# Order of the query and key loads on SP's line, and the row length of these loads, in a two-block transformer kernel on one core

## What is computed

```python
q = jnp.einsum('oc,bct->bot', Wq, target) + bq[None, :, None]
k = jnp.einsum('oc,bcs->bos', Wk, source) + bk[None, :, None]
v = jnp.einsum('oc,bcs->bos', Wv, source) + bv[None, :, None]
q = q.reshape(b, HEADS, HEAD_DIM, t)
...
dot = jnp.einsum('bhdt,bhds->bhts', q, k) / math.sqrt(HEAD_DIM)
dot = mask * dot - (1.0 - mask) * NEG
amap = jax.nn.softmax(dot, axis=-1) * mask
out = jnp.einsum('bhts,bhds->bhdt', amap, v)
...
x = x + jnp.tanh(g_xattn[0]) * out
```

## Time and profile before

| | us |
|---|---|
| median of 3 runs (1378.74 to 1382.11) | 1381.76 |
| the profiled execution | 1371.15 |
| its span | 1369.3 |
| PE busy / DVE busy / ACT busy / POOL busy | 1113.3 / 1033.2 / 668.1 / 523.4 |
| DMA queue of SP, share of 16 engines over the span | 38.8% |
| attention, about | 158 to 645 |

### The profile page before, as it was taken

One profiled execution on the slowest core, in us unless ns is written; L12 is line 12 of the kernel. 1 busy time (PEld: TensorE's weight loads), 2 busy tenths in 40 slices (PEclk: granted clock), 3 DMA queues, 4 the chain that ended last, 5 costly groups with the idle time before them and its releaser, 6 DMA issues. The chain is left out here.

```text
span 1369.3 us, 16346 instructions
## 1 busy us (share of the span) xinstructions
PE 1113.3 (81%) x4725; PEld 447.5 (33%) x4802; DVE 1033.2 (75%) x1587; ACT 668.1 (49%) x783; POOL 523.4 (38%) x384
## 2 busy tenths in 40 slices
PE   0887279998879987983799998599999999259777
PEld 0443112222222222220344444344444444134232
DVE  5765488887767877751799997388788887767898
ACT  0355308776657766684466665211000000386796
POOL 0466601244332442355011111477888787000021
PEclk9999659999989999997999999799999999579889
DMA  7398797677756776621311110111111111000011
GB/s 266 127 338 319 199 146 83 119 153 108 125 90 124 151 111 115 114 71 58 151 47 46 40 36 16 35 62 62 62 62 50 58 62 46 1 0 0 0 62 62
DMA packets 84274, 129.33 MB, mean 94 GB/s; under 512 B 13544, under 2 KB 53864, under 8 KB 83696
## 3 DMA queue, kind: packets, MB, share of 16 engines
q1 hardware_dynamic: 84224, 128.72, 38.8%
HBM read 104.44 MB, written 21.89 MB: 92 GB/s over the span
## 5 line engine op out<-in xcount | busy, mean ns | idle before, releaser
L793 DVE TENSOR_REDUCE mneg<-ps_m 128x1 f32<-128x512 f32 x512 | 322.2, 683 | 93.8 <-PE ps_m L707 78.3
L1337 PE MATMUL ps_y<-kv,toeplitz_sb 128*128 128x512 f32 x640 | 279.6, 596 | 8.7 <-POOL kv L1249 8.7
L675 ACT ACTIVATE probs<-ps_s 128x1024 f32<-128x1024 f32 x256 | 249.9, 1022 | 51.9 <-PE ps_s L728 51.9
L707 PE MATMUL ps_m<-k_stack,q_stack 128*128 128x512 bf16 x489 | 181.9, 410 | 55.3 <-DMA k_stack<-mask_k 50.4
L1337 PEld LDWEIGHTS ps_y<-kv,toeplitz_sb 128*128 128x128 f32 x640 | 121.1, 191 | 155.0 <-issue 155.0
L728 PE MATMUL ps_s<-q_stack,k_stack 128*128 128x512 bf16 x492 | 151.0, 387 | 21.1 <-ACT probs L675 11.2
L738 PE MATMUL ps_o<-probs,v_all 128*17 128x512 f32 x1024 | 140.1, 620 | 0.4 <-ACT probs L675 0.4
L1249 POOL TENSOR_TENSOR kv<-vT,ctxT_sb 128x2048 f32<-128x2048 f32 x32 | 118.7, 3711 | 40.0 <-PE ps_y L1337 32.6
L972 PE MATMUL ps_g<-w,xT_f 128*128 128x512 bf16 x491 | 116.7, 384 | 8.4 <-DVE h_f L1119 6.6
L623 POOL TENSOR_TENSOR inv_all<-inv_all,mb_b 128x512 f32<-128x512 f32 x16 | 20.4, 1274 | 254.9 <-DMA inv_all<-inv_rows 254.9
L707 PEld LDWEIGHTS ps_m<-k_stack,q_stack 128*128 128x128 bf16 x512 | 42.2, 99 | 219.4 <-DVE mneg L793 104.5
(11 more groups left out here) (163 smaller groups left out, 1662.6 us busy)
## 6 DMA issues: line engine op xcount, KB each, us to landing
w_sweep<-in_w SPq DMA_DIRECT2D x8, 1536.0 KB, 8.5
q_stack<-q_parts SPq DMA_DIRECT2D x96, 128.0 KB
k_stack<-k_parts SPq DMA_DIRECT2D x96, 128.0 KB
w_sweep<-in_w SPq DMA_DIRECT2D x16, 768.0 KB, 6.5
w_sweep<-in_w SPq DMA_DIRECT2D x16, 512.0 KB, 3.3
toeplitz_sb<-in_toeplitz SPq DMA_DIRECT2D x32, 256.0 KB, 2.6
w_f<-in_w SPq DMA_DIRECT2D x32, 256.0 KB, 2.9
q_parts<-qk_part SPq DMA_DIRECT2D x24, 256.0 KB, 4.0
```

The lines of the kernel that those rows point to most:

```text
L675: nc.scalar.activation(pr[:, k % 2, 2 * slot:2 * slot + 2, :], S[:, 2 * slot:2 * slot + 2, :], ACT.Exp).then_inc(exp_done, 1)
L707: nc.tensor.matmul(M[:, bank(j), :], Q[:, slot, hd, tc * P:(tc + 1) * P], K[:, slot, hd, :], start=True, stop=True).then_inc(max_mm, 1)
L793: nc.vector.tensor_reduce(mneg[:, h, tile % LT, tile // LT:tile // LT + 1], M[:, bank(j), :], AX.X, ALU.max, negate=True).then_inc(max_red, 1)
L1337: mm = nc.tensor.matmul(Y[:, q % 3, l2, :], T[:, g % 2, (lt - m) * P:(lt - m + 1) * P], kv[:, g % 2, m, :], start=(m == 0), stop=(m == lt))
```

## The change

Two things. First, SP no longer issues the load of unit u+2 at the start of unit u's turn; at the end of unit u's turn it issues that of unit u+3. The prologue now loads units 0, 1 and 2, the last between the two weight loads. SP's loop over batches is written out instead of run as a loop. Second, the host orders the columns of `wqT` and `wkT` and the biases so that within each 128 channels the channel of head h and dimension d is 8d + h instead of 16h + d. A partition's eight heads then lie in `q_parts` as one run of 8 KB, and a block's load reads 16 such runs; before it read 128 rows of 1 KB. What lies in `Q` and `K` afterwards is the same.

```diff
@@ load_unit
-                                         s.rearrange("a (h d) l -> d (a h) l", d=HD)).then_inc(qk_loaded[slot], 16)
+                                         s.rearrange("a (d h) l -> d (a h) l", d=HD)).then_inc(qk_loaded[slot], 16)
...
                 load_batch(0, 0)
                 load_weights(0, 0)
+                load_unit(1, 2, 0, fresh=True)
                 load_weights(1, 1)
-                sp.wait_ge(zeroed[2], 2)
-                sp.wait_ge(zeroed[3], 2)
                 place_max(0, 0, 0)
...
                 def batch(b, par, first, last):
                     for h in range(2):
                         u = 2 * b + h
-                        if not last:
-                            if not first:
-                                sp.wait_ge(scores_done, 2 * STEPS * (u - 1))
-                            load_unit(b + 1, 2 * (1 - par) + h, h)
...
                             load_weights(u + 1, 1 - h)
+                        if u + 3 < 2 * B:
+                            if u:
+                                sp.wait_ge(scores_done, 2 * STEPS * u)
+                            load_unit((u + 3) // 2, (u + 3) % 4, (u + 3) % 2, fresh=u == 0)
...
-                over_batches(sp, batch)
+                for b in range(B):
+                    batch(b, b % 2, b == 0, b == B - 1)
...
+    def by_dim(v):
+        return np.ascontiguousarray(v.reshape(v.shape[:-1] + (CT, P // HD, HD)).swapaxes(-1, -2).reshape(v.shape))
...
-        "wqT": np.ascontiguousarray(inputs["L0_xattn_Wq"].T), "wkT": np.ascontiguousarray(inputs["L0_xattn_Wk"].T),
+        "wqT": by_dim(inputs["L0_xattn_Wq"].T), "wkT": by_dim(inputs["L0_xattn_Wk"].T),
```

More of the change, by code:

```diff
@@ L1810 @@
         "x": arr("x"), "ctx": arr("ctx_2048"), "mask": arr("mask_Bx1x2048_fk1"), "g_xattn": arr("g_xattn"),
-        "g_ffn": arr("g_ffn"), "bq": columns(inputs["L0_xattn_bq"]), "bk": columns(inputs["L0_xattn_bk"]),
+        "g_ffn": arr("g_ffn"), "bq": columns(by_dim(inputs["L0_xattn_bq"])), "bk": columns(by_dim(inputs["L0_xattn_bk"])),
         "mask_cols": np.ascontiguousarray(inputs["mask_Bx1x2048_fk1"].reshape(B, LT, P).transpose(2, 0, 1)),
         "bv": arr("L0_xattn_bv"),
-        "wqT": np.ascontiguousarray(inputs["L0_xattn_Wq"].T), "wkT": np.ascontiguousarray(inputs["L0_xattn_Wk"].T),
+        "wqT": by_dim(inputs["L0_xattn_Wq"].T), "wkT": by_dim(inputs["L0_xattn_Wk"].T),
         "wvT": np.ascontiguousarray(inputs["L0_xattn_Wv"].T),
```

## The result

The changed kernel takes 1394.12 us (median of 4 runs, 1387.31 to 1398.13), the kernel before 1381.22 on the same chip (median of 4, 1378.74 to 1382.11): a ratio of 1.0091 with a 95% interval of [1.0049, 1.0133]. It is slower, by 12.9 us of medians. The profiled execution took 1387.31 us, the shortest of the four, with a span of 1385.5, against 1371.15 and 1369.3: 16.2 us between the spans. Where they lie is read in order of time.

What follows compares the result with a forecast made beforehand. No engine is full; PE waits for unit loads, up to 48 us. Terms +7.6 - 1.0 + 1.7 + 0 = +8.3 took 1371.15 to 1379.4, 1390 us carried to the median; range 1384 to 1397, 8-in-10 1368 to 1412.

Steps and rivals of the forecast that it cites:

- its own signs of being wrong: Forecast wrong if the load's rate leaves 115 to 130 GB/s, or the prologue's wait is under 4 us.
- From unit 3's load on, no DMA of SP passes another. Price: nothing.: SP's order: only unit 2's load really moves, in the prologue; later order, issue and the written-out loop cost nothing.
- The wait for unit 0's maxima, +7.6: Before unit 0's first scores: PE waits 7.6 us for maxima queued behind unit 2's load, seen at 212.3 against 204.75.
- 1.70 MB at the 121 GB/s of unit 0's and 1's loads: Prologue: unit 2's load, ahead of unit 0's maxima, takes 14.1 us at this rate, so rings are empty at 210.6.
- covered: Rival, chance 0.12: unit 0's maxima find free rings, leaving only -1.0 us, 1381 us; against it, masks and weights use every ring.
- Unit 0's wait for unit 2's load gone, -1.0: In unit 0: the wait at 216.59 vanishes, its step of 3.82 us becoming 2.81, a gain of 1.0 us.
- The clock, +1.7: Behind PE's wait before unit 0's scores: the clock drops as after waits above 2.2 us, costing 1.7 us.
- Rows of 8 KB, 0: In every unit's load: the span of 16 partitions limits the rate, so longer rows change nothing, 0 us.
- rows were the limit: Rival, chance 0.06: in the loads, 8 KB rows take 9.3 us off each, total -58.5 us, 1323 us.
- rows help a little: Rival, chance 0.17: in the loads, engines drift over more blocks, -0.9 us a load, total -8.6 us, 1373 us.
- Rows hurt: Rival, chance 0.17: in the loads, coarser packets put all engines in one block, +1.6 us each, total +40.8, 1423 us.
- The shift is kept.: In the later units: loads hang on unit 1's maxima, which move with PE, so the prologue's delay stays; no size added.

Runs made afterwards that it cites:

- experiment 2: Changed kernel with the second weight load, unit 2's masks, or both weight loads issued behind unit 0's maxima: 1.0109, 1.0119 and 1.0072 of the kernel before.
- maxima_first: Changed kernel with unit 2's load put back behind the second weight load and unit 0's maxima: 1.0028 of the kernel before.
- both_weights_behind: Changed kernel with both of the prologue's weight loads issued behind unit 0's maxima: 1.0072 of the kernel before.
- masks_behind: Changed kernel with only unit 2's two mask transfers issued behind unit 0's maxima: 1.0119 of the kernel before.
- spread_rows_first: Changed kernel with each block's rows on every sixth of 96 partitions and unit 2's load behind unit 0's maxima: 0.9578 of the kernel before.

## Why the prediction was right, and where its sum was not

The forecast of 1390 us, slower, was right in sign and mechanism: 12.9 us of medians against a sum of 8.3, 1394 inside its own range of 1384 to 1397. How near the number came owes something to luck: its main term was half of what was measured, the trace shows 16.2 us in all, and 4.2 us that came back over the twelve units can't be put down to the change. Of its own signs of being wrong, the load's rate comes to the bound of 115 GB/s for units 0 and 1, and to 111 from 200.5 to 214.5, unit 2's load with some rows of the weights beside it. The terms:

- **"From unit 3's load on, no DMA of SP passes another. Price: nothing."** Held: with unit 2's load put back, everything else of the change (issue, written-out loop and rows) gives 1.0028, 0.5% at most.
- **The wait for unit 0's maxima, +7.6.** The mis-sized term: 14.1 measured, 15.0 with what stands around it. The step that failed is "1.70 MB at the 121 GB/s of unit 0's and 1's loads". By that sum, with attention starting 2.5 us later, the rings would have been through 14.1 us behind 199.0 and the maxima seen at 214.8; it was 222.25, 7.4 us late (PE was itself ready only at 208.1, which is why the wait grew by 6.5).
  - What the runs showed of these 7.4 us: the mean over 16 rings isn't the time of those that the maxima use. By the reading of experiment 2, the slow half begins its long rows at 200.5, not 199.0 (+1.5). They and the masks take until 218.0, 17.5 us instead of 14.1 (+3.4). By an estimate from the 7.1 GB/s an engine of this kernel's own loads, twelve rows of 8 KB take 13.8 us and the masks' 16 KB 2.3 more. The second weight load, now behind the load, takes until 221 (+3.0), and the maxima and their landing 1.25 us instead of 1.7.
  - Taken away one at a time in the experiments, the masks gave 2.4 us, the second weight load 2.5, the first 1.0, and the long rows 1.1. "The masks' eight rows and the weights pass over every ring", in the rival "covered", doesn't fit the masks.
  - What stays open: in the forecast the weights' time lies before 199.0, at nearly four times the load's rate, so their bytes alone don't make them late; why the slow half lags that far, no run took apart.
  - That the maxima's two rows share a ring with the masks is argued from their place at the end, not shown. The Trainium skill ("DMA: Bandwidth & Descriptors", Why a DMA increments its semaphore by 16 and not by 1) puts a DMA whose sides divide into k rows on the lowest k of 16 rings; that would put the masks' eight and the maxima's two on the same ones.
- **Unit 0's wait for unit 2's load gone, -1.0.** Wrong, it was worth nothing. The step of 3.82 us was put down to the wait of 0.41. In the changed kernel that wait is gone and the step is 3.77 (235.31 to 239.08): the time goes to the transposes of the maxima (L716), which wait for DVE's last maximum. The wait on the load lay beside that.
- **The clock, +1.7.** Held: unit 0's first four steps take 13.1 us (222.25 to 235.31) where they took 10.8 (204.75 to 215.59), +2.2; the steps are 3.4 and 4.1 us at first, and 2.8 from the third on, and the granted clock was 0.62 in the first 8 us instead of 1.00. Part of it is no matter of the wait: in `maxima_first`, which has none, the four steps take 11.8 us (204.35 to 216.15).
- **Rows of 8 KB, 0.** Held within what can be told: 1.0021 alone; the loads at 115 instead of 119 GB/s in the same window; packets of 1.15 us where 1.2 was forecast. The rivals "rows were the limit" and "rows help a little" fall. "Rows hurt" leans the right way, at a fraction of its 32 us: the wait is 14.1 against 13.0.
- **"The shift is kept."** Mostly: of the 17.0 us lost by 264.96 (beside the later start), 4.2 came back over twelve units, since the waits sank from 36.2 to 31.7 us. Among kernels that differ from the changed one in the prologue alone these sums run from 32.5 (`both_weights_behind`) to 38.1 us (`masks_behind`), and their twelve units from 329.3 to 338.5 us, so I don't put it down to the change.
- **"The stall is covered" (rival, 0.12).** Refuted: on SP's queue the maxima's packets are the last to go, and on a queue of their own none goes for 10.5 us.

What the prediction said of the stage and had no lever for was the larger thing: 23.9 us for a unit without waits, and up to 48 us that hang on the loads. With loads at nearly twice the rate the first came out to the tenth and the second at 48.5 us, for 4% of the kernel.

## What to carry to other kernels

A small DMA that the critical engine waits for costs the whole backlog of its own rings, not of their mean, and here a queue of its own took only 2.6 us off: look at what is issued ahead of it before "issue the prefetch earlier". Where a load writes 16 neighbouring partitions at a time, neither longer rows nor an earlier place helped here; let its rows go to partitions that lie further apart (every second already took the rate from 121 to 213 GB/s), if what reads them doesn't mind, and look whether the issue of the DMAs is the next limit. And before a wait in a step is priced by the step's length, see in the timeline which engine's work ends last in it.

## What the runs showed of the hardware that was not expected

- A DMA of 16 KB on ACT's queue got its first packet 10.5 us after its issue, while the 16 engines worked on SP's queue at 114 GB/s into blocks of 16 partitions. Then it shared them, 18 packets among 163 in 3.7 us.
- Two transfers that alternate in the same 32 partitions reach 213 GB/s, two that follow each other in blocks of 16 get 121, with the same bytes and packets. Going from 32 to 64 partitions added nothing (206), with the engines busy all the time in both.
- Of 16 engines that work on one queue, some end several us before the others: in the changed kernel the last 3 us before unit 0's maxima pass at a share of 0.45.
- Rows of 8 KB gained nothing that shows where the partitions allow more, either: 193 GB/s with the engines busy 0.95 of the time (`spread_rows_first`), against 227 at 1.06 with rows of 1 KB. The queues weren't equally full in these windows, so that they are slower isn't shown.
